# Reciprocals one step sooner, the head reordered, and the queries loaded from SyncE's queue behind the keys

## What is computed

```python
h = _layernorm(x, axis=-1) * (1 + ca) + sa
latent = h @ Wc_down
q = (latent @ Wq_up).reshape(B, T, 16, 8)
kv = latent @ Wkv_up
k, v = kv[..., :8], kv[..., 8:]
att = jnp.einsum('bthd,bsd->bhts', q, k) / sqrt(8)
att = jax.nn.softmax(where(causal, att, -inf), axis=-1)
y = jnp.einsum('bhts,bsd->bthd', att, v).reshape(B, T, 128)
x = x + ga * (y @ Wc_proj)
```

## Time and profile before

| | us |
|---|---|
| median of 3 runs | 884.55 |
| lowest and highest of them | 882.77, 1658.92 |
| profiled execution, its own time | 880.3 |
| its span | 878.5 |
| layer 0's attention, about | 0 to 386 |
| experts and layer 1 | 386 to 878.5 |

### The profile page before, as it was taken

How to read it: one execution, slowest core, us unless ns; L and a number is a source line. 1 busy time by engine, 2 the same in 40 slices (tenths; PEclk the granted TensorE clock), 3 DMA queues, 4 the chain that set the end, 5 groups by cost and what they waited for, 6 DMA issues and landing times.

```text
span 878.5 us, 22949 instructions
## 1 busy us (share of the span) xinstructions
PE 730.9 (83%) x9158; PEld 390.1 (44%) x9158; DVE 554.5 (63%) x1483; ACT 449.5 (51%) x742; POOL 416.9 (47%) x554
## 2 busy tenths in 40 slices
PE   4587998889898898948889999879947699999887
PEld 2234444444444443423434444434424356656555
DVE  4876686868676693457681343302387688887884
ACT  2013675657575566613134333333346588888663
POOL 6022133624435233110046888887545669885333
PEclk9655999999999999969999898889968899999999
DMA  6621464355442422240012333333300111111001
GB/s 165 130 57 31 99 171 98 79 142 150 94 101 75 110 75 65 86 133 1 0 29 49 43 44 41 44 43 34 48 24 2 25 27 25 38 27 26 21 19 37
DMA packets 73923, 55.06 MB, mean 63 GB/s; under 512 B 23698, under 2 KB 66818, under 8 KB 73218
## 3 DMA queue, kind: packets, MB, share of 16 engines
q1 hardware_dynamic: 63098, 36.58, 16.2%
q0 software_dynamic: 9856, 7.58, 6.6%
q10 hardware_dynamic: 864, 9.44, 5.0%
HBM read 31.76 MB, written 18.23 MB: 57 GB/s over the span
## 4 chain that ended last, share of the span: by engine, by line
PE 28%; POOL 21%; DVE 14%; issue 13%; DMA 10%; SPq 8%; ACT 5%; POOLq 1%; DVEq 0%; ACTq 0%
POOL d_acc L1381 9%; POOL XG L1371 4%; PE b1ps L2075 3%; PE b1ps L2086 3%; POOL xn L976 3%; DMA d_r<-rc 3%; PE ps_s L423 2%; DMA K<-d_k 2%; PE b1ps L2099 2%; DVE MX L794 2%; PE bank L439 2%; SPq L1088 2%; PE bank L462 2%; DVE hit L1415 2%; SPq L1102 1%
## 5 line engine op out<-in xcount | busy, mean ns | idle before, releaser
L649 ACT ACTIVATE PR<-ps_s 128x1024 f32<-128x1024 f32 x160 | 155.6, 1021 | 111.8 <-PE ps_s L419 79.0
L794 DVE TENSOR_REDUCE MX<-bank 128x1 f32<-128x320 f32 (+13 forms) x352 | 180.9, 561 | 44.9 <-PE bank L469 41.7
L462 PE MATMUL bank<-K,Q 72*32 72x32 bf16 (+15 forms) x2048 | 121.6, 311 | 22.1 <-DMA K<-d_k 16.1
L423 PE MATMUL ps_s<-Q,K 97*32 97x512 bf16 (+1 forms) x1088 | 99.6, 395 | 5.0 <-DMA Q<-d_m 4.3
L1381 POOL DMA_INDIRECT d_acc<-Y,idx x56 | 87.7, 1566 | 21.8 <-issue 16.5
L462 PEld LDWEIGHTS bank<-K,Q 72*32 72x32 bf16 x2048 | 49.6, 104 | 101.6 <-DVE MX L794 41.2
L1585 PE MATMUL ps_o<-H,w 128*128 128x512 f32 x176 | 91.5, 672 | 0.0
L1371 POOL DMA_INDIRECT XG<-d_tab,idx x56 | 54.2, 968 | 78.3 <-DVE idx L1486 61.8
L439 PE MATMUL bank<-PR,VE 128*32 128x512 f32 x640 | 85.5, 611 | 0.0
L1705 ACT ACTIVATE H<-ps_h,b1T 128x512 f32<-128x512 f32 x88 | 60.3, 687 | 41.5 <-PE ps_h L1573 39.3
L469 PE MATMUL bank<-maskQ,identb 128*32 128x32 bf16 (+3 forms) x1408 | 73.0, 200 | 0.8 <-issue 0.8
(11 more groups left out here) (347 smaller groups left out, 1390.2 us busy)
## 6 DMA issues: line engine op xcount, KB each, us to landing
Q<-d_q ACTq DMA_DIRECT2D x24, 384.0 KB
d_q<-qs SPq DMA_DIRECT2D x24, 128.0 KB, 2.4
X<-L_attn_x SPq DMA_DIRECT2D x8, 256.0 KB, 5.0
w<-L_ffn_W SPq DMA_DIRECT2D x8, 256.0 KB, 4.0
d_acc<-zrow SPq DMA_DIRECT2D x1, 2048.0 KB, 10.3
w<-L_ffn_W SPq DMA_DIRECT2D x1, 2048.0 KB, 9.7
AC<-d_acc SPq DMA_DIRECT2D x8, 256.0 KB, 2.9
d_y<-ysb SPq DMA_DIRECT2D x112, 18.0 KB
```

Of the source, the lines that this page charges most:

```text
L423: last = nc.tensor.matmul(out_, k_[0:r, P * i + o:P * i + o + QW], q_[0:r, :, P * g + QW * j:P * g + QW * j + QW], start=True, stop=True, ...
L462: nc.tensor.matmul(mx[o:o + QW, x * w:(x + 1) * w], Q[b % QB][0:NPR, 4 * c + hh, QW * j:QW * j + QW], K[b % QB][0:NPR, 0:w], start=(x == 0 ...
L649: nc.scalar.activation(by_head.rearrange("p h (c x) -> p c h x", x=QW), ps_s[half][:, :].rearrange("p (c h x) -> p c h x", c=2, x=QW), ACT ...
L794: nc.vector.tensor_reduce(MX[b % 2][:, c:c + len(cs)], ring[R0.place["max", G]][:, 0:len(cs) * w].rearrange("p (x w) -> p x w", w=w), AX_X ...
```

## The change

Four edits, all in layer 0's attention:

1. The three loads of Q leave ACT's list. SP issues them in the same step 4, behind the three loads of K, and waits for `q_st` there.
2. The reciprocals: DVE takes them in step 2, before the first split of k, and not in step 3. SP stores them at the head of step 3, before the stores of q and k, and loads `rl` behind these stores, still in step 3 and before the second y_store.
3. DVE clears Q2 at the start, right behind Q0, and no longer after `modulation_rows`. The counts that the loads wait for follow that (1, 3, 3).
4. The limit rows of buffers 1 and 2 wait until the first block's Q and K have landed.

```diff
--- before.py
+++ after.py
@@ -656,16 +656,6 @@
                         y_out(NT * b + g)
                 for kind, b in misc_at(n, s):
                     misc(kind, b)
-                b = n + 2
-                if 0 <= b < NB and s == 4:
-                    par = b % 2
-                    act.wait_ge(DS[f"q_st{par}"], 48 * (b // 2 + 1))
-                    if b < QB:
-                        act.wait_ge(s_qz, b + 1)
-                    for c in range(PARTS):
-                        act.dma_start(Q[b % QB][24 * c:24 * c + 24].rearrange("r h q -> r (h q)"),
-                                      bass.AP(d_q[par].tensor, 0, [[NH * T, PARTS * DH], [1, NH * T]])
-                                      ).then_inc(DS[f"q_in{par}"], 16)
                 if (s == 8 and 0 <= n - 2 < LB - 2) or (n, s) in ((LB, 5), (NB, 0)):
                     b = n - 2
                     act.wait_ge(S["misc_free"], M0.full(("lg", b)))
@@ -884,6 +874,7 @@
                     if b == 0:
                         modulation_columns()
                         clear(Q[0])
+                        clear(Q[2])
                 b = n - 2
                 if 0 <= b < LB - 1 and s == 0:
                     dve.wait_ge(S["misc_free"], M0.full(("pj", b)))
@@ -891,7 +882,7 @@
                         dve.wait_ge(S["xn2_rdy"], b)
                     norm_stats(X[:, NT * b:NT * b + NT, :], stat2, mv2, S["mv2_rdy"])
                 b = n - 1
-                if 0 <= b < LB and s == 3:
+                if 0 <= b < LB and s == 2:
                     dve.wait_ge(DS["lc_in"], 16 * (b + 1))
                     if b >= 1:
                         dve.wait_ge(DS["r_st"], 16 * b)
@@ -940,7 +931,6 @@
                     block_mask()
                     clear(Q[1])
                     modulation_rows()
-                    clear(Q[2])
                 b = n - 2
                 if 0 <= b < LB - 2 and s == 9:
                     gates(b, 0, NT, tab).then_inc(S["tab_rdy"], 1)
@@ -1092,6 +1082,12 @@
         for n in range(-LEAD, NB + TAIL):
             for s in range(NSTEP):
                 t = NSTEP * n + s
+                if 0 <= n - 1 < LB and s == 3:
+                    b = n - 1
+                    sp.wait_ge(S["rc_rdy"], b + 1)
+                    if b >= 2:
+                        sp.wait_ge(DS["rl_in"], 16 * (b - 1))
+                    sp.dma_start(d_r[b % 2].rearrange("h (a q) -> (h a) q", q=64), rc[:, :]).then_inc(DS["r_st"], 16)
                 b = n + 2
                 if 0 <= b < NB and s == 3:
                     par = b % 2
@@ -1105,6 +1101,11 @@
                     for i in range(NT):
                         sp.dma_start(bass.AP(d_k[par].tensor, P * i, [[T, DH], [DH * T, PARTS], [1, P]]),
                                      ks[32 * i:32 * i + DH, :, :]).then_inc(DS[f"k_st{par}"], 16)
+                if 0 <= n - 1 < LB and s == 3:
+                    b = n - 1
+                    sp.wait_ge(DS["r_st"], 16 * (b + 1))
+                    sp.dma_start(rl[:, :], bass.AP(d_r[b % 2].tensor, 0, [[T, NH], [0, DH], [1, T]])
+                                 ).then_inc(DS["rl_in"], 16)
                 b = n + 2
                 if 0 <= b < NB and s == 4:
                     par = b % 2
@@ -1112,6 +1113,13 @@
                     for c in range(PARTS):
                         sp.dma_start(K[b % QB][24 * c:24 * c + 24, :],
                                      bass.AP(d_k[par].tensor, c * DH * T, [[0, PARTS], [T, DH], [1, T]])
+                                     ).then_inc(DS[f"q_in{par}"], 16)
+                    sp.wait_ge(DS[f"q_st{par}"], 48 * (b // 2 + 1))
+                    if b < QB:
+                        sp.wait_ge(s_qz, (1, 3, 3)[b])
+                    for c in range(PARTS):
+                        sp.dma_start(Q[b % QB][24 * c:24 * c + 24].rearrange("r h q -> r (h q)"),
+                                     bass.AP(d_q[par].tensor, 0, [[NH * T, PARTS * DH], [1, NH * T]])
                                      ).then_inc(DS[f"q_in{par}"], 16)
                 if 0 <= t - 1 < NSTEP * NB:
                     b, ps = divmod(t - 1, NSTEP)
@@ -1130,17 +1138,11 @@
                                  ).then_inc(DS["lc_in"], 16)
                     sp.dma_start(yt[:, :], bass.AP(y.tensor, 0, [[(DH + 1) * T, NH], [T, DH], [1, T]])
                                  ).then_inc(DS["yt_in"], 16)
-                if 0 <= b < LB and s == 4:
-                    sp.wait_ge(S["rc_rdy"], b + 1)
-                    if b >= 2:
-                        sp.wait_ge(DS["rl_in"], 16 * (b - 1))
-                    r = d_r[b % 2]
-                    sp.dma_start(r.rearrange("h (a q) -> (h a) q", q=64), rc[:, :]).then_inc(DS["r_st"], 16)
-                    sp.wait_ge(DS["r_st"], 16 * (b + 1))
-                    sp.dma_start(rl[:, :], bass.AP(r.tensor, 0, [[T, NH], [0, DH], [1, T]])).then_inc(DS["rl_in"], 16)
                 if (n, s) in LIMIT_ROWS:
                     i = LIMIT_ROWS.index((n, s))
                     sp.wait_ge(s_eye, 1)
+                    if i >= 1:
+                        sp.wait_ge(DS["q_in0"], QIN)
                     sp.dma_start(K[i][NPR:P, :], KC[:, :]).then_inc(s_kc[i], 16)
                     sp.dma_start(Q[i][P - QW:P, :, :], bc(QC[:, :].unsqueeze(1), [QW, NH, T])).then_inc(s_kc[i], 16)
                 if n == -1 and s == 3:
```

## The result

Measured: median **903.97 us** of 4 runs (900.28 to 910.18); the kernel before, run beside it, 884.13 of 4. The ratio is 1.0196 with a 95% interval of 1.014 to 1.0251: slower, by about 2%. A ratio here is estimated from the single executions of both kernels and is not the quotient of the two medians. The profiled execution took 900.28 us, its span was 898.5 (before 880.3 and 878.5), its mean granted clock 0.901 (before 0.907). The forecast was 876, the range 862 to 897: the time lies 7 us above the range, at the place where rival B had put it (900).

What follows compares the result with a forecast made beforehand. PE was taken to set the pace, waiting for late yn, with loads landing just when wanted. From 880.3 us, −14.6 + 9.4 − 0.5 − 3.0 = −8.7 gave 871.6, for the median 876; range 862 to 897.

Steps and rivals of the forecast that it cites:

- rival B: PE's first group of maxima, step 8: Q takes 10.8 us from its own later issue; +15.4, 900 us; 16%.
- Queries on SP: Q's loads issued by SP behind K land later, paid in the rounds loading blocks 1 to 7; +9.4 us.
- the shift: Later landing of Q before PE's step 8: +1.6 us a round in blocks 3 to 7, 0.7 in blocks 1 and 2.
- its own two bounds: Limits for Q's later landing: +4.4 us if its own issue counts, 0 if only the end of contention counts.
- Reciprocals: Sooner reciprocals and store of rc let yn run earlier, removing PE's waits for yn and one gap; −14.6 us.
- Clock: PE's half-speed drops behind the four yn gaps above 2 us, half counted as gone; −3.0 us.
- Head: First block: early memset frees DVE, Q issued later but not sharing engines with limit rows; −0.5 us.
- A: Loads not late at all: Q lands as early as before; −24 us, 861 us; 15%.
- C: Maxima's store and load of cb, behind Q on SP's queue, become the wait; 6 us lost, 882 us; 9%.
- D: Nothing moves: another wait, such as a free bank, takes up what yn leaves; 884 us; 8%.

Runs made afterwards that it cites:

- experiment 2: Kernel before with only Q's loads moved to SP, behind K in step 4; 904.7 us, ratio 1.0248.
- experiment 5: Changed kernel with Q's loads on ACT's own queue, but in step 5; 909.61 us, ratio 1.0213.
- experiment 6: Changed kernel loading only half of every row of Q in blocks 3 to 7 (wrong numbers); 882.25 us, ratio 0.9879.
- experiment 1: Changed kernel with Q's loads back on ACT in step 4; 875.58 us, ratio 0.9896.
- experiment 7: Changed kernel with Q's loads on ACT in step 4 and rl's load behind K's; 881.22 us, ratio 0.9874; repeated 877.6 us, 0.9859.
- experiment 3: Kernel before with the reciprocals' part alone, Q on ACT and head as before; 879.77 us, ratio 0.9938.
- experiment 8: Kernel before with the head's part alone (early third clear, limit rows behind the first loads); 889.02 us, ratio 0.9963.

## Why the prediction was wrong

**The step that failed is "Queries on SP"**, in the term of the shift. The prediction set +1.6 us a round where the round of the earlier trace rows measured +4.4, the upper of its own two bounds. It had the issue right: 8.1 us behind the store of q (214.5 less 206.37), measured 8.02. What it had wrong is what follows: 7.9 to 8.4 us to landing, against 10.97 measured. It gave Q 0.9 us to start and 7 us to move, and left the tail of 3 us at a share of 0.20 to K. The packets of the kernel before show 0.9 us and 8.2 us: Q's rows moved until 219.18, well into that tail, and only the 1.2 us from there to 220.41 were K's alone (K's rows had not moved before 218.58). In the changed kernel it was 1.1 us to start, 8.9 to move, and 1.0 from the last row to PE's start, which the working had left out. That K, being ahead, would have left the engines was right: its rows ended at 225.81, and the time behind Q's last row fell from 1.8 to 1.0 us. Q's slower transfer took that back (9.1 to 10.0 us from the issue). What slowed it is not shown; the load of cb, 192 KB, and the maxima's store now stand right behind Q's issue. Experiments 2 and 5 show 11.0 and 11.5 us on two queues, and experiment 6 that most of the time follows Q's bytes.

Over the eight blocks the term was +9.4 plus the head's −0.5, and 29.4 was measured: 23.2 in blocks 3 to 7 (forecast 8.0), 4.8 in blocks 1 and 2 (1.4), 1.4 in the head (−0.5). Rival B had 22, 6 and 2. Block 7 alone takes 7.3; one profile does not say why. Against the forecast for the profiled execution, 871.6 us, the 900.28 measured are 28.7 more: 20.5 by this term, 6.6 by reciprocals and clock together, 1.6 in the unchanged part.

**Reciprocals** (−14.6): the mechanism is right. yn starts 7.3 us behind the store of q (223.15 less 215.89; before 18.2, 224.58 less 206.37), PE's waits for it are gone, and DVE does not wait for lc in these rounds. The store of rc lands as soon as forecast (median of the page, 6.7 us before):

```profile
d_r<-rc SPq DMA_DIRECT2D x7, 32.0 KB, 1.7
```

Only in the first of these rounds SP stands for rc: q is ready at 130.74 and stored at 131.64. The term is still too large, for a reason it did not name: rl's load now stands ahead of K and Q, and with it there the pair took longer to land (experiments 1 and 7), and the limits became a wait as well (experiment 1). Alone the edit brings 0.6% (experiment 3), with the head and with rl behind K 1.4% (experiment 7).

**Clock** (−3.0): it did not come, it turned round. The gaps of 2.5 to 3.6 us for yn became gaps of 3.4 to 6.8 us for Q. In the five rounds that load blocks 3 to 7 PE's clock stood at 0.50 for 17 us in sum before and for 31 us after. PE's busy time in the attention, for the same 5770 matmuls, rose by 2.0 us instead of falling by 3.0:

```profile
0.00:386.40 386.40, 316.17 (x5770) 157.44 (x5770) 263.63 (x681) 198.20 (x250) 129.66 (x233) 0.89 0.41 100
...
0.00:404.76 404.76, 318.14 (x5770) 156.49 (x5770) 263.35 (x681) 198.53 (x250) 129.33 (x233) 0.88 0.39 95
```

Reciprocals and clock together were −17.6; the second parts of the loop shrank by 11.0.

**Head** (−0.5): +1.4 in the first block. Q's first issue came at 28.32 instead of 25.19, behind K's loads on SP, and the cleared tile was early to no use: DVE, done with it, waits for PE instead.

```profile
15.80 3.47 DVE L674 MEMSET Q<- 32x4096 f32 x1 [0.80 <-issue]
...
38.25 0.29 DVE L784 TENSOR_REDUCE MX<-bank 128x4 f32<-128x128 f32 x1 [5.13 <-PE bank L469]
```

**Rivals.** A had no support in any run. C was no wait of PE's: PE waited once, 3.3 us, for the limits, where it had waited 4.3 before. But half of its mechanism came. Issued behind Q, the maxima's store took much longer to land than the 1.97 us that C had counted (median of the page, 2.0 before):

```profile
d_m<-ms SPq DMA_DIRECT2D x24, 16.0 KB, 4.9
```

In the five rounds that load blocks 3 to 7 the first of its three parts landed 4.8 to 7.5 us behind its issue, within about 0.5 us of the moment when Q was there. PE did not stand for it, since PE itself stood for that same Q. The Trainium skill ("DMA: Bandwidth & Descriptors", on queues, rings and completion order), whose rule spoke for C, says that an engine takes one ring in order and alternates between rings. The first half agrees with these rows. The second does not show: in the kernel before, K's rows on another queue were held until 218.58, when nearly all of Q was through. So sharing the queue is not needed to hold the store either: in experiment 5, with Q on ACT's queue and the store on SP's, the same part took 5.3 to 6.0 us in these rounds and landed within 0.7 us of Q too. C's wait grew where Q was not moved, to 9.9 us in experiment 1. D's idea, that another wait takes up what yn leaves, is what experiments 1 and 8 show in part. B is what happened: 900 forecast, 903.97 measured, its price 30 less 14.6, the account 29.4 less 11.0, and 1.6 elsewhere. That B came so near is in part luck: it took Q's 10.8 us as one fixed time, while K's rest went out of it and a slower Q came in.

The chances were wrong for the same reason as the sum. B had 16% though the trace showed eight loads that all landed 10.0 to 11.3 us behind ACT's issue; the one reason against it was a share of 0.20 in a window of 3 us, and Q's own packets ran until 219.18, into that window.

## What to carry to other kernels

When a large load is moved, first take its time from issue to landing in each round of the trace; if that is nearly constant and the consumer waits close behind it, each microsecond of later issue is a microsecond of the loop; here it was so on both queues. Which load lands last, and how long each takes, is read from their packets; a mean share of the engines does not tell it. Issue the largest transfer first (here Q, then K, then rl), and count among the things moved ahead of it the bytes as well as the issues. Removing a wait is worth what the next-latest arrival allows: here the loads landed just when they were wanted, so the same edit was worth 0.6% alone and, with the head and with rl out of the loads' way, 1.4%.

## What the runs showed of the hardware

- Three loads of 24 rows, 1.18 MB in all, took 10.0 to 11.3 us from first issue to PE's start in the eight blocks of the kernel before, on ACT's queue, and in five of eight blocks of the changed one, on SP's, 10.0 to 11.0 (the others 9.5, 9.6 and 12.9). Their own rows took 8.4 to 9.7 us from the issue to the end of the last before and 8.3 to 11.4 after. Half the bytes took 6.7 to PE's start. The same bytes in nine loads of 8 rows took 20.1.
- K's 72 rows of 1 KB, issued 0.5 to 2.7 us behind Q on another queue, moved within 1.3 to 2.6 us at the end, behind nearly all of Q, in six of blocks 1 to 7 of the kernel before. Issued ahead of Q they began to move 1.5 us behind their issue.
- With a load of 256 KB issued 0.1 us ahead of them, and K 1.2 us later, it was 15.1 us; with that load behind K, 12.2 (means of blocks 3 to 7: 12.7 and 11.4).
- A store of 32 KB took 7.25 us to land beside these loads and 1.7 issued ahead of them (medians 6.7 and 1.7). A store of 16 KB issued behind them took 4.8 to 7.5 us to land on their queue and 5.3 to 6.0 on the other, against 2.1 to 2.4 with the loads landed (the rounds that load blocks 3 to 7).
- PE's granted clock was at 0.50 until 5.8 us behind the end of a gap of 4.26 us (234.88 to 240.7), and until 4.6 us behind the end of one of 2.56 us (226.10 to 230.7). It stayed at 1.00 behind one of 0.86. The cost of it is at most about 2 us a round.
